# First attention: three score buffers, one bank for all side work, and VectorE's norm chain ahead of the router's counts

## The reference

```
x = x + attn_a(layernorm(x))       # 16 heads of 8; q and k divided by their norms; softmax(g_scale * q k^T) v
x = x + moe(layernorm(x))          # 8 experts, top 2, capacity, 128 -> 512 -> 128
x = x + attn_b(layernorm(x))       # 16 heads of 64, relative position bias
x = x + moe(layernorm(x))

def attn_a(x):                     # the stage that is changed
    q, k, v = (x @ W.T).reshape(B, S, 16, 8).transpose(0, 2, 1, 3) for each of the three W
    q = q / max(norm(q), EPS); k = k / max(norm(k), EPS)
    attn = softmax(g_scale * einsum('bhqd,bhkd->bhqk', q, k))
    return einsum('bhqk,bhkd->bhqd', attn, v)
```

## Time and profile before

| what | value |
|---|---|
| median of 3 runs | 1417.54 us (1417.42 to 1420.83) |
| profiled execution, its own time | 1409.33 us |
| profiled execution, its span | 1407.6 us |
| granted TensorE clock over the span | 0.956 |
| first exponential of the first attention starts | 37.7 us |
| last one starts | 348.0 us |
| exponentials in it | 256, median 1.114 us each |

### The profile page before, as it was taken

The page is one execution under the profiler, slowest core; times in us unless marked ns, Lnnn a source line. Parts: engine busy times, 40 slices in busy tenths (PEclk is TensorE's granted clock), DMA queues, the critical chain, the costliest instruction groups (busy, mean ns, idle before and its releaser), DMA issues. The chain is left out here.

```text
span 1407.6 us, 22606 instructions
## 1 busy us (share of the span) xinstructions
PE 1252.3 (89%) x6739; PEld 642.7 (46%) x6739; DVE 937.7 (67%) x2837; ACT 873.8 (62%) x1716; POOL 512.5 (36%) x788
## 2 busy tenths in 40 slices
PE   2899999999396899999999999999999999997492
PEld 1333344333273344544544644544544544545271
DVE  5346656654212787798798798799798798785110
ACT  1799988898041766666666576577567567662040
POOL 2000323224464233233443433433533533434255
PEclk7799999999698999999999999999999999999696
DMA  5564444336953466576676576567576666678222
GB/s 155 128 211 147 134 141 142 132 128 205 198 73 59 105 142 145 142 170 145 145 173 155 134 169 164 132 166 162 131 168 148 136 162 141 141 162 217 70 23 22
DMA packets 132936, 197.91 MB, mean 141 GB/s; under 512 B 35166, under 2 KB 76077, under 8 KB 132816
## 3 DMA queue, kind: packets, MB, share of 16 engines
q1 hardware_dynamic: 104848, 138.67, 38.6%
q0 software_dynamic: 27392, 56.76, 19.3%
q10 hardware_dynamic: 576, 1.05, 0.2%
HBM read 61.75 MB, written 39.24 MB: 72 GB/s over the span
## 5 line engine op out<-in xcount | busy, mean ns | idle before, releaser
L1694 ACT ACTIVATE tile<-tile,low 128x512 f32<-128x512 f32 x512 | 363.5, 714 | 239.3 <-DVE low L1780 239.1
L1470 POOL DMA_DIRECT2D crossed<-blocks x512 | 254.0, 504 | 478.8 <-DVE blocks L1793 436.1
L1780 DVE CUSTOM_DVE_ANT_0 tile<-s_ps,bias 128x512 f32<-128x512 f32 x512 | 330.6, 682 | 41.8 <-PE s_ps L1557 34.8
L681 ACT ACTIVATE probs_a<-score_ps,gbound 128x1024 f32<-128x1024 f32 x256 | 272.2, 1114 | 53.8 <-PE score_ps L962 53.5
L1557 PE MATMUL s_ps<-kT,qT 64*128 64x512 f32 x1024 | 260.1, 619 | 15.1 <-DVE low L1780 13.4
L1793 DVE STREAM_TRANSPOSE blocks<-tile 128x512 f32<-128x512 f32 x384 | 256.8, 694 | 0.0
L1577 PE MATMUL o_psb<-crossed,v_b 128*64 128x512 f32 x512 | 235.6, 603 | 10.0 <-DMA crossed<-blocks 8.9
L389 POOL DMA_INDIRECT slots<-rows_r,slot_r x128 | 128.1, 1001 | 65.7 <-issue 50.6
L1557 PEld LDWEIGHTS s_ps<-kT,qT 64*128 64x128 f32 x1024 | 85.2, 185 | 134.0 <-issue 85.6
L962 PE MATMUL score_ps<-q_stack,k_stack 32*128 32x512 f32 x512 | 123.3, 503 | 18.4 <-DMA q_stack<-q_parts 14.0
L975 PE MATMUL o_ps<-probs_a,v_ext 128*32 128x512 f32 x1024 | 136.8, 608 | 1.3 <-DVE o_sb L794 1.3
(11 more groups left out here) (188 smaller groups left out, 1647.7 us busy)
## 6 DMA issues: line engine op xcount, KB each, us to landing
crossed<-blocks SPq DMA_DIRECT2D x512, 96.0 KB
crossed<-blocks POOLq DMA_DIRECT2D x512, 96.0 KB
inv_row<-inv_rows SPq DMA_DIRECT2D x128, 128.0 KB, 4.4
q_parts<-parts SPq DMA_DIRECT2D x32, 256.0 KB, 3.8
k_stack<-k_parts SPq DMA_DIRECT2D x32, 256.0 KB, 3.4
q_stack<-q_parts SPq DMA_DIRECT2D x32, 256.0 KB, 4.3
w_f<-in_w SPq DMA_DIRECT2D x32, 256.0 KB, 5.9
k_parts<-parts SPq DMA_DIRECT2D x28, 256.0 KB, 3.6
```

The costliest lines, as they stand in the source:

```text
L681: nc.scalar.activation(probs[q % 2][:, c % 4 // 2, pair:pair + 2, :].rearrange("p h t -> p (h t)"), score_ps[c % 2][:, :], ACT.Exp, bias=g ...
L1470: pool.dma_start(strip_to(n, a, m), strip_from(n, a, m)).then_inc(crossed_sw[n % 2], 16)
L1694: nc.scalar.activation(tile[(b * NS + k) % RING][s][:, :], tile[(b * NS + k) % RING][s][:, :], ACT.Exp, bias=low[n % 2][:, s, i:i + 1], sc ...
L1780: nc.vector.tensor_tensor_reduce(out=tile[(b * NS + k) % RING][s][:, :], in0=s_ps[k % 2][s][:, :], in1=bias[:, h, off:off + S], scale=1.0, ...
```

## The change

Three score buffers take the place of two; `aux_ps` and `t_ps` are gone, and all side work goes through one bank, `side_ps`. TensorE now goes by pairs of chunks: four score matmuls in a row, on the four groups of 32 rows and into four banks, then at most one piece of side work, then a `values` call. The scores of a pair wait for the exponential of the chunk two before the pair's first. Since `side_ps` has one bank, q and k are made in two halves, each copied by VectorE into `qk_unit` (new, L773 after); ScalarE squares them from there; they are scaled in place; q and k are turned and split one after the other. Each user of the bank waits until the one before has been read. VectorE's order is new: the norm chain of b+1 stands ahead of the router's `run_counts` and `weigh`. The end of the stage uses the score buffers for the router's last work. In `MORE` and `LAST` the numbers are pairs of chunks; "tokens-1" is the last group of the batch before, "q" and "k" are `turn_qk`, and -1 and -2 at the router's names are batches before.

```diff
-        score_ps = [ps(f"score_ps{n}", 2 * S) for n in range(2)]
-        aux_ps = ps("aux_ps", 2 * S)
+        score_ps = [ps(f"score_ps{n}", 2 * S) for n in range(3)]
         o_ps = ps("o_ps", S)
-        t_ps = ps("t_ps", S)
+        side_ps = ps("side_ps", S)
...
-        SQUARE_AT = 5
-        TURN_X, QK_FIRST, QK_SECOND, MAKE_V, TURN_QK = 0, 2, 4, 6, 16
-        TOKENS_MORE, TOKENS_LAST = {10: -1, 18: 0, 22: 1, 30: 2}, {6: -1, 14: 0, 22: 1, 30: 2}
-        ROUTE_MORE = dict(counts=22, turn=26, logits=28, exps=30)
-        ROUTE_LAST = dict(counts=8, turn=18, logits=20, exps=22, own_counts=28)
+        MORE = {0: "x", 1: "qk0", 2: "qk1", 3: "tokens-1", 6: "v", 7: "tokens0", 8: "q", 9: "k",
+                11: "tokens1", 12: "counts-2", 13: "turn-1", 14: "logits-1", 15: "tokens2"}
+        LAST = {3: "tokens-1", 4: "counts-2", 7: "tokens0", 9: "turn-1", 10: "logits-1", 11: "tokens1",
+                14: "counts-1", 15: "tokens2"}
+        EXPS_MORE, EXPS_LAST, SQUARE_AT = 30, 23, 6
...
+                for n in range(2 if b >= 1 else 1):
+                    for own, ready in enumerate((hi_ready, rest_ready)):
+                        wait(sp, ready, b, n + 1)
+                        sp.sem_inc(g["passed_sp"], 1)
+                        for other in range(2):
+                            dram = (q_dram[:, other, own], k_dram[:, own, other])[n]
...
-                wait(act, qk_ps, b, 1)
-                nc.scalar.activation(squares[:, :], aux_ps[:, :], ACT.Square).then_inc(sq_ready.sem, 1)
+                wait(act, qk_copied, b, 2)
+                nc.scalar.activation(squares[:, :], qk_unit[:, :, :].rearrange("p t d -> p (t d)"), ACT.Square).then_inc(sq_ready.sem, 1)
...
+            def take_qk(b, half):
+                wait(dve, qk_ps, b, half + 1)
+                wait(dve, qkT_ps, 0, 2 * b)
+                nc.vector.tensor_copy(qk_unit[:, 2 * half:2 * half + 2, :].rearrange("p t d -> p (t d)"),
+                                      side_ps[:, :]).then_inc(qk_copied.sem, 1)
+
+            def high_part(b, n):
+                wait(dve, qkT_ps, b, n + 1)
+                wait(dve, parts_out, 0, b * parts_out.per)
+                nc.vector.tensor_copy(parts[:, 0, n, :], side_ps[:, :]).then_inc(hi_ready.sem, 1)
+
+            def low_part(b, n):
+                wait(dve, hi_ready, b, n + 1)
+                nc.vector.tensor_tensor(parts[:, 1, n, :], side_ps[:, :], parts[:, 0, n, :].bitcast(F32),
+                                        ALU.subtract).then_inc(rest_ready.sem, 1)
+
+            def split(b, n):
+                high_part(b, n)
+                low_part(b, n)

             def statistics(lo, hi, n):
...
             def batch(b):
                 prepare(b + 1, 1)
                 if b >= 2:
                     r.pick(dve, b - 2, 0)
+                take_qk(b + 1, 0)
+                if b >= 1:
+                    take(b - 1, 3)
+                take_qk(b + 1, 1)
+                if b >= 2:
                     r.pick(dve, b - 2, 1)
                 if b >= 1:
-                    take(b - 1, 3)
+                    finish(b - 1, 3)
+                prepare(b + 1, 3)
+                prepare(b + 1, 4)
+                take(b, 0)
+                prepare(b + 1, 2)
+                prepare(b + 1, 5)
+                finish(b, 0)
                 if b >= 2:
                     r.run_counts(dve, b - 2)
+                split(b + 1, 0)
+                if b >= 2:
                     r.weigh(dve, b - 2)
-                prepare(b + 1, 3)
-                prepare(b + 1, 2)
-                prepare(b + 1, 4)
-                take(b, 0)
-                prepare(b + 1, 5)
+                high_part(b + 1, 1)
+                take(b, 1)
+                low_part(b + 1, 1)
                 if b >= 1:
-                    finish(b - 1, 3)
                     wait(dve, res_done, b - 1, GROUPS)
                     r.norm_stats(dve, b - 1)
-                prepare(b + 1, 6)
-                take(b, 1)
+                    r.norm_moments(dve, b - 1)
+                finish(b, 1)
                 if b >= 1:
-                    r.norm_moments(dve, b - 1)
-                finish(b, 0)
+                    r.norm_rows(dve, b - 1)
                 if b >= 2:
                     r.take_counts(dve, b - 2, counts)
-                    r.address(dve, b - 2)
-                if b >= 1:
-                    r.norm_rows(dve, b - 1)
-                finish(b, 1)
                 if b >= 1:
                     r.copy_turned(dve, b - 1, turned)
                 take(b, 2)
+                if b >= 2:
+                    r.address(dve, b - 2)
                 if b >= 1:
                     r.shift(dve, b - 1, logits)
...
-            for stage in (0, 1, 3, 4, 5, 2, 6):
+            prepare(0, 0)
+            prepare(0, 1)
+            take_qk(0, 0)
+            take_qk(0, 1)
+            prepare(0, 2)
+            for stage in (3, 4, 5):
                 prepare(0, stage)
+            split(0, 0)
+            split(0, 1)
...
+            def make_qk(b, half):
+                if half == 0:
+                    wait(pe, xT_ready, b, 1)
+                else:
+                    wait(pe, qk_copied, b, 1)
+                for i in range(2):
+                    tile = 2 * half + i
+                    last = nc.tensor.matmul(side_ps[:, i * 2 * D:(i + 1) * 2 * D], xT[:, tile * P:(tile + 1) * P],
+                                            w3[:, 0:2 * D], start=True, stop=True)
...
+                if n == 1:
+                    wait(pe, rest_ready, b, 1)
+                elif b >= 1:
+                    wait(pe, on_step, b - 1, 2)
+                else:
+                    wait(pe, v_staged, 0, 1)
+                for i in range(TB):
+                    last = nc.tensor.transpose(side_ps[:, i * P:(i + 1) * P],
+                                               qk_unit[:, i, n * D:(n + 1) * D], g["ident"][:, :])
...
-            def scores(b, c, before):
-                q, kt = c // 4, c % 8 // 2
-                grp = q // 2
-                if c % 8 == 0:
+            def scores(b, pair, before):
+                first = 2 * pair
+                grp = first // 8
+                if first % 8 == 0:
                     wait(pe, stacks_in[grp], b, 16 * 2)
-                if c >= 2 or before:
-                    wait(pe, p_ready, b, c - 1)
-                elif c == 1:
+                if first >= 2 or before:
+                    wait(pe, p_ready, b, first - 1)
+                else:
                     pe.wait_ge(table_sb, 2)
-                for n in range(2):
-                    r = 32 * (2 * (c % 2) + n)
-                    last = nc.tensor.matmul(score_ps[c % 2][:, n * S:(n + 1) * S],
-                                            k_stack[b % 2][r:r + 32, grp, kt * P:(kt + 1) * P],
-                                            q_stack[b % 2][r:r + 32, grp, :], start=True, stop=True)
-                last.then_inc(s_ready.sem, 1)
+                for c in (first, first + 1):
+                    kt = c % 8 // 2
+                    for n in range(2):
+                        row = 32 * (2 * (c % 2) + n)
+                        last = nc.tensor.matmul(score_ps[(b * NCH + c) % 3][:, n * S:(n + 1) * S],
+                                                k_stack[b % 2][row:row + 32, grp, kt * P:(kt + 1) * P],
+                                                q_stack[b % 2][row:row + 32, grp, :], start=True, stop=True)
+                    last.then_inc(s_ready.sem, 1)
 
...
+                if what == "tokens0":
+                    to_tokens(b, 0, lambda: wait(pe, v_staged, b + 1, 1))
+                if what == "q":
+                    turn_qk(b + 1, 0)
+                if what == "k":
+                    turn_qk(b + 1, 1)
+                if what == "tokens1":
+                    to_tokens(b, 1, lambda: wait(pe, rest_ready, b + 1, 2))
...
-                tokens_at = TOKENS_MORE if more else TOKENS_LAST
-                for q in range(8):
-                    for part in range(4):
-                        c = 4 * q + part
-                        scores(b, c, before)
-                        if part % 2 == 1:
-                            if q >= 1:
-                                values(b, q - 1, part // 2)
-                            elif before:
-                                values(b - 1, 7, part // 2)
-                        if more:
-                            extras(b, c)
-                        if c in tokens_at:
-                            tokens(b, tokens_at[c])
-                        if b >= 2 and c == at["counts"]:
-                            r.counts(pe, b - 2, counts, lambda: wait(pe, rest_ready, 0, min(b + 2, B)))
-                        if before and c == at["turn"]:
-                            r.turn(pe, b - 1, turned, lambda: wait(pe, rest_ready, 0, min(b + 2, B)))
-                        if before and c == at["logits"]:
```

(13 more changed lines are left out.)

184 lines of the change are left out of this document (88 added, 96 removed).

## The result

The changed kernel takes 1395.16 us (median of 4 runs, 1391.07 to 1399.79), the kernel before 1417.48 beside it (4 runs, 1406.66 to 1420.83). The ratio is 0.9879, with a 95% interval from 0.9844 to 0.9913: faster by 1.2%. On another chip, later, it was 1389.12 against 1406.57, ratio 0.9877 [0.985, 0.9904].

What follows compares the result with a forecast made beforehand. TensorE was taken as the bound (busy 39.52 of 40 us), ScalarE next. Savings of 5 x 3.0 + 3.5 + 3.2 + 0 = 21.7, taken as 21, bring 1417.54 to 1396.5 us; range 1383 to 1410, the walk alone 1390 to 1402.

Steps and rivals of the forecast that it cites:

- Four score matmuls in 0.44: TensorE, each pair: four score matmuls on different row groups overlap and together take 0.44 us, within bounds 0.43 to 0.86.
- A steady batch of 36.0 by the walk: Batches 2 to 6: following each pair's waits between engines gives 36.0 us instead of 39.0, saving 3.0 each.
- Batch 1 saves 3.5: Batch 1: no router counts come between, so k's turn does not wait; saves 3.5 us.
- Stacks at 29.8, no wait: Next batch's q and k stacks: first issued at 29.8 us, landed by 34.5, wanted at 36.0; cover 1.5 us.
- Ahead of the first batch, 0 in sum: Prologue: first exponential 0.6 to 1 us later, but batch 0 gains later what it loses there; 0 in sum.
- its own sign: Prologue: the prediction is wrong there if the first exponential starts outside 38 to 39 us.
- The last batch saves 3.2, "I find no wait in it that lasts": Last batch, first to last exponential: 34.6 us falls to ScalarE's pace of 31.4, saving 3.2.
- the 31.4 of the sum: Last batch: its exponentials at ScalarE's pace need 31 x 1.01 + 0.1 = 31.4 us.
- Sum 21: Whole kernel: the batch savings add to 21.7 us, taken as 21 for semaphores in waits left out.

Runs made afterwards that it cites:

- e1: Changed kernel with three score buffers kept, but a pair's two chunks issued apart, the second behind the side work: 1418.67 us, ratio 1.0072 to the kernel before.
- e6: Changed kernel with four banks for batch 0's prologue instead of one, and v copied behind batch 0's norm chain: 1386.78 us, ratio 0.985 to the kernel before.
- e8: e7 with the last two scatters of batch 4 issued ahead of batch 6's inverse deviation on GpSimd: 1382.05 us, ratio 0.9811 to the kernel before.
- e9: Changed kernel with only GpSimd's order exchanged, batch 4's last two scatters ahead of batch 6's inverse deviation: 1388.46 us, beside 1389.12 unaltered.
- e4: Changed kernel with v made at pair 5 instead of 6 and copied by VectorE ahead of `take` of group 0: 1383.92 us in one run.
- e3: Changed kernel with VectorE's `run_counts` and `weigh` put back in front of the norm chain: 1393.58 us in one run.
- e7: e5 and e6 joined: v at pair 5, VectorE's changed order and the four-bank prologue; 1378.42 us, ratio 0.9805 to the kernel before.
- e5: e4 with VectorE's order changed as well (router's second pick, `run_counts`, scaling and split moved forward): 1386.34 us, ratio 0.9845 to the kernel before.
- e8_again: e8's kernel run once more, on the same chip as the unaltered changed kernel: 1379.08 us, ratio 0.98 to the kernel before.
- e2: Changed kernel with two score buffers instead of three, a pair's four matmuls waiting for both exponentials in front: 1478.9 us, ratio 1.0489 to the kernel before.

## Why the prediction was right

It said 1396.5 us and the median was 1395.16. That they lie so near is in part luck: the saving was 22.3 us there and 17.5 on another chip, for the 21 forecast, and the time behind the stage varies by 10 us from one profile to the next. The stage is the better test. The steps, one by one:

- **Four score matmuls in 0.44.** Right: 0.43. The Trainium skill (TensorE: Matmul & The Clock Gate, Part 3: Packing small matmuls, Measured speedup vs the span model) has 3.07 times for four row tiles, by which an estimate is 0.56. The trace doesn't agree: four take what two took, and what one takes. (One by one, the four bias matmuls of the prologue, 32 rows and 512 columns too, start 0.43 apart in the kernel before: 1.89 us for four, the last of which takes 0.59.) e1 shows that this term carries the gain.
- **A steady batch of 36.0 by the walk.** Right: 36.02 in the mean of five (35.79 to 36.41), and 35.81 in the second profile. Five saved 15.0 us, as said. Q's turn waits 0.45 (0.6 said), k's 0.59 (0.8), `o_ps` 0.46 (0.4). The reduction starts 9.6 us behind pair 0's scores (9.6), v's copy ends at 16.0 (16.0), the scaling at 18.5 (18.7). Pairs 1, 2, 8 and 9 take 2.41, 2.49, 2.51 and 2.65 us on ScalarE where the pairs without a wait take 1.99: losses of 0.4, 0.5, 0.5 and 0.7 where 0.4, 0.5, 0.6 and 0.8 stood. One term was too small and makes up for that: behind the router's logits, pair 14 takes 2.42, a loss of 0.4 and not 0.1.
- **Batch 1 saves 3.5.** Right: 3.65 in the first profile.
- **Stacks at 29.8, no wait.** Right: 29.65.
- **Ahead of the first batch, 0 in sum.** Right in sum, by luck: batch 1 begins at 79.37 us for 79.52. But the prologue failed its own sign: the first exponential starts at 39.46, outside of the 38 to 39 that I gave, 1.8 us later than before and not 0.6 to 1; batch 0 happened to give back as much (39.91 for 41.85). The reduction starts at 18.20 and not 16.7, and the other batches' statistics at 29.79, 4.5 us later than before where I said 2.7. What I had mis-sized: the two halves of q and k put v's start off by 2.3 us (15.48 for 13.17), where I counted two copies of 0.7, and v's eight matmuls took 2.08 us, where I counted 0.7 to 0.9 and the kernel before took 1.05. e6 brings the reduction back to 15.44, by the banks and by the place of v's copy.
- **The last batch saves 3.2, "I find no wait in it that lasts".** This is the term that was mis-sized: 1.5 in the first profile and 2.1 in the second. The first profile has a wait whose cause is open (below). In the second there was one hidden before, since all else was slower: the landing of two scatters, 15.9 to 18.2 us into the batch, against a turn that is due at 17.7 and, in the kernel before, came at 19.2. With it out of the way (e8, e9) the last batch takes 31.36 and 31.37, the 31.4 of the sum.
- **Sum 21.** The last exponential moved by 20.4 us, the medians by 22.3 on one chip and 17.5 on another.

One thing stays open. In the first profile of the changed kernel `norm_rows` was in time, and yet ScalarE waited 1.75 us for nothing that the trace names:

```profile
294.54 22.22 ACT L680 ACTIVATE probs_a<-score_ps,gbound 128x1024 f32<-128x1024 f32 x22 [0.17 <-PE score_ps L997]
318.51 2.12 ACT L680 ACTIVATE probs_a<-score_ps,gbound 128x1024 f32<-128x1024 f32 x2 [1.75 <-remote]
```

Its scores had started at 316.23 us. e4 has the like of it in the same pair (1.95 us), the other profiles not. So this unexplained wait is what the last batch missed its 31.4 by in the first profile (1.7 us), and the landing in the second (1.15). In e3 and e6 that pair took 4.40 us with the granted clock at 0.50; here and in e4 it took 4.02 and 4.07 with the clock given as 1.00. I can't tell whether these are one thing.

## What to carry to other kernels

Where matmuls use 32 rows of the array, issue those on different row groups back to back before anything else: it took 0.43 us of TensorE's work off a pair and 3.2 of 39 us off a batch, and it needs one more score buffer than the pair to be worth anything (with two buffers it cost 4.9%, apart over three 0.7%). When a stage gets faster, list the transfers that don't: a landing that doesn't come earlier with it becomes the wait. And price a matmul in a prologue at both rates that the rows show for it; here these were 1.05 and 2.08 us.

## What the hardware showed that I had not expected

- In the prologue v's projection took 2.08 us, against 1.05 for the same matmuls in the kernel before and 1.16 in the steady batches. Yet busy time by stretch gives the granted clock as 1.00 there:

```profile
16.00:36.00 20.00, 7.28 (x20) 3.11 (x18) 15.38 (x58) 1.64 (x3) 1.01 (x4) 1.00 0.44 132
```

A half of q and k takes 2.08 us too (9.76, shown above), to the hundredth what it takes in the kernel before at a granted clock of 0.50 (first fence). And four score matmuls take 0.80 us at 44.68 in the changed kernel, at a granted clock of 1.00 (second fence), for 0.51 in the steady batches:

```profile
41.07 2.08 PE L927 MATMUL aux_ps<-w,xT_a 128*128 128x256 f32 x4
```

```profile
44.68 0.80 PE L997 MATMUL score_ps<-q_stack,k_stack 32*128 32x512 f32 x4
```

So up to some 47 us of this execution, a granted clock of 1.00 stands beside matmuls that take the time of 0.50 (1.2 GHz): it does not show by itself that they run at 2.4 GHz. The wait in front of v is not what makes it slow: in e7, where v follows q and k without one, it takes 1.92 us, and in e6, the same there, 1.41.

```profile
13.36 1.92 PE L969 MATMUL o_ps<-w,xT_a 128*128 128x128 f32 x8
```
- In the last batch the granted clock fell to 0.50 (1.2 GHz) in four profiles of those in which TensorE waited over 1 us for `norm_rows`: for 17.1 us in e1 (idle 1.68 us before), 10.2 in e3 (1.28), 10.2 in e6 (2.21), 3.4 in e7 (1.63), each time within a microsecond of the end of the idle time. It stayed at 1.00 in two more, the second profile of the changed kernel (1.14) and e4 (2.09), and in those without such a wait (before, the changed kernel's first, e5, e8, e9 and e8_again), except in e2, whose clock falls all through the stage. So the length of the wait doesn't decide it alone. Where the clock fell for 10 us or more, in e1, e3 and e6, pairs 9 to 11 took 8.8, 6.2 and 6.8 us over their 6.0, for a wait of 1.68, 1.28 and 2.21.
- Two scatters issued 2.3 us earlier let `norm_rows` start 4.2 us earlier (e9). Where the trace has their landings, it comes 4.1 and 3.7 us behind the issue in e9, and 5.1 and 6.5 us in e6, which issues them 2.3 us later. A scatter of the same batch, issued before the next stage's loads begin 7.7 us into the batch, takes 2.1. So beside these loads a small transfer's landing hangs on more than its issue. That it is the loads that hold it up is my reading; no run took them away.
